# A layer of causal attention gated by an expert mixture: gating the last batch after the last head, weighing and gating on other engines, and adding the causal mask on VectorE

## The chip, the cores and the metric

The program runs on one core of one Trainium2 chip, in one launch. The metric is the device time of a launch in microseconds (us). The kernel before took 1059.01 us, the median of three runs (1058.56, 1059.01 and 1065.69). All times in the text are us unless marked ns.

A core has five engines with in-order streams that wait for each other only by semaphores: TensorE (PE; matmuls, results in PSUM), VectorE (DVE), ScalarE (ACT), GpSimd (POOL) and SyncE (SP, here a queue of DMAs). GpSimd can't reach PSUM.

## The reference, cut to what matters

```python
xn = layernorm(x)                              # x: 4 batches x 1024 tokens x 256
q  = (xn @ Wq + bq)  -> 8 heads of 128; k, v = xn @ Wkv + bkv    # one k, v for all heads
q, k += sinusoidal positions
scores = q k^T / sqrt(128); masked above the diagonal
s  = softmax(scores) v  -> 1024 x 1024, @ Wo   -> 1024 x 256 per batch
logits = xn @ router_w + router_b; the two largest of 8 experts are kept
f  = sum over the two kept experts of gate_e * (relu(xn @ w1[e] + b1[e]) @ w2[e] + b2[e])
out = x + s * silu(f)
```

## The kernel before, in words

**Two stages.** The first (to about 479 us) makes the layernorm, the routing and the eight experts; the experts' rows lie in device memory as `expert_outputs`. The second, `attention`, is the one that the change touches. It runs over 32 heads (4 batches x 8), n = 0 to 31. A token tile is 128 tokens; c = 0 to 31 are the tiles of all batches, c = 24 to 31 those of the last batch (`TILES` = 24).

**A head has five steps**, k = 5n + i. `GROUPS` says which query tiles u a step takes: (7), (6, 0), (5, 1), (4, 2), (3). Tile u needs (u + 1) x 128 columns of scores, so a head has eight blocks of 1024, 896 + 128, 768 + 256, 640 + 384 and 512 columns. The order of each engine's stream is written out by hand in loops over k:

- TensorE: `scores` (three matmul passes of f16 parts, and for the diagonal block a fourth matmul, L1346, that adds the mask: identity x `maskb`), then `values` of the head before, then in steps 0 and 2 a job (`project`, the q of head n + 2), and in step 4 `o_tile`, the output projection of tile n - 9. Heads 30 and 31 have no job.
- VectorE: `o_gated` (step 0, L1608), `job_positions` (L1551), `reciprocals` (L1571), `o_low` (steps 0 and 3, L1587), `maxima` (L1542), `job_low` (L1565), `low` of two steps back (L1581), and then `whole_f` (step 2, L1593) and `gated` (step 4, L1602).
- ScalarE: `job_high` (L1473), `high` of the step before (L1483), `expo` (L1453, with an accumulator read behind each block), `o_high` (steps 2 and 4, L1461), `weigh` (step 1, L1491) and `tanh` (step 3, L1509).
- GpSimd: `added` (step 1, L1664) and `fetch` (step 3, L1658), two indirect DMAs that gather the two expert rows of each token of a tile.
- SyncE: the transposing DMAs of the probabilities' two f16 parts, and loads and stores of x.

**Gating one tile** takes: `fetch` (two gathers), `weigh` (f = gate0 x row0), `whole_f` (f += gate1 x row1), `tanh` (of f / 2), `gated` (G = (tanh + 1) x f), `o_gated` (G x the tile's output projection) and `added` (+ x). `yg` has three buffers, `fb`, `thb` and `Gb` two. Before, the order `seq` takes the last batch's eight tiles first, one in each of heads 1 to 8 (they rest in `GD`), then tiles 0 to 23 in heads 9 to 31 and one behind the last head. The last batch's output projection is made after the last head in four PSUM banks (`rows_out`, L1399), multiplied by `GD` in `closing` (L1635), added to x and stored.

## Time and profile before

| | before |
|---|---|
| median of 3 runs | 1059.01 us |
| the profiled execution's own time | 1065.57 us |
| its span, first to last instruction | 1063.7 us |
| TensorE busy, share of the span | 992.4 us, 93% |
| VectorE busy | 859.3 us, 81% |
| ScalarE busy | 647.2 us, 61% |
| GpSimd busy | 339.2 us, 32% |
| mean granted TensorE clock | 0.996 |

The page's shares are means over the two stages, whose limits differ, so the stretches of the attention stage are read one by one. A "head" is counted below from the start of one reduction over 1024 columns (step 0) to the next. A row's duration of an instruction overlaps the next one's start by some 0.1 us on VectorE and ScalarE; where the text speaks of a step, it is the distance from start to start.

### The profile page before, as it was taken

How to read it: one execution, taken by the hardware profiler on the slowest of the kernel's cores; microseconds unless marked ns; L12 is line 12 of the kernel's file. 1: busy time of each engine (PE TensorE's matmuls, PEld its weight loads, DVE VectorE, ACT ScalarE, POOL GpSimd, SP SyncE). 2: the span in 40 equal slices, each digit the busy share in tenths (PEclk: the TensorE clock that was granted, in tenths of full speed). 3: DMA queues.
4: the chain of work that ended last, by engine and by line, in shares of the span. 5: the costliest groups of instructions: out<-in, count | busy, mean ns of one | idle time of the engine just before them, and what ended most of it. 6: DMA issues, size and time to landing. Idle time of an engine off the chain costs nothing.

```text
span 1063.7 us, 25358 instructions
## 1 busy us (share of the span) xinstructions
PE 992.4 (93%) x8590; PEld 774.2 (73%) x8590; DVE 859.3 (81%) x1529; ACT 647.2 (61%) x1370; POOL 339.2 (32%) x350
## 2 busy tenths in 40 slices
PE   0797999999999999999988989999999999999997
PEld 0565888888888888886655656777777777777776
DVE  6986578787676546559999999999999999999972
ACT  2743233333332333338888988888888888888860
POOL 3104899899997300002110101212121111212111
PEclk9999899999999999999999999999999999999999
DMA  8777687768775522218989999999999998999992
GB/s 277 228 287 154 164 204 191 203 179 198 175 174 160 155 46 67 62 45 187 178 158 188 159 159 170 190 185 187 173 185 180 188 179 174 168 161 164 180 176 91
DMA packets 428269, 179.46 MB, mean 169 GB/s; under 512 B 363850, under 2 KB 417940, under 8 KB 427380
## 3 DMA queue, kind: packets, MB, share of 16 engines
q1 hardware_dynamic: 364272, 131.39, 60.5%
q10 hardware_dynamic: 57396, 28.74, 11.4%
q0 software_dynamic: 6480, 17.70, 6.4%
q8 instruction: 77, 1.26, 0.5%
q14 instruction: 44, 0.36, 0.1%
HBM read 54.94 MB, written 34.87 MB: 84 GB/s over the span
## 4 chain that ended last, share of the span: by engine, by line
PE 36%; DVE 11%; ACT 4%; issue 3%; ACTq 0%; DVEq 0%
PE b_psS L1343 11%; PE b_psO L1371 11%; PE b_psJ L1388 5%; PE b_psJ L1302 5%; DVE b_ph L1581 4%; DVE b_nmax L1542 4%; PE b_psS L1399 2%; ACT b_pr L1453 2%; ACT b_ph L1483 1%; PE b_psO L1374 1%; DVE b_psJ L1551 1%; PE b_psS L1346 1%; DVE b_Q L1565 1%; DVE b_outs L1587 1%; ACT b_outs L1461 0%
## 5 line engine op out<-in xcount | busy, mean ns | idle before, releaser
L1005 PE MATMUL psU<-bxT,w_p 128*128 128x256 f16 (+1 forms) x1920 | 288.0, 262 | 10.7 <-DMA bxT<-expert_rows 4.9
L1096 ACT ACTIVATE h<-psU,bias 128x256 f32<-128x256 f32 (+1 forms) x320 | 123.9, 449 | 257.4 <-PE psU L1005 205.2
L1014 PE MATMUL psY<-w_p,hp 128*128 x1704 | 274.9, 274 | 0.1
L1343 PE MATMUL b_psS<-b_kp,b_Q 128*128 128x512 f16 (+3 forms) x1152 | 218.6, 326 | 12.3 <-ACT b_pr L1453 10.8
L1453 ACT ACTIVATE b_pr<-b_psS,b_nmax 128x1024 f32<-128x1024 f32 (+7 forms) x256 | 187.0, 735 | 43.9 <-DVE b_nmax L1542 42.9
L1005 PEld LDWEIGHTS psU<-bxT,w_p 128*128 x1920 | 187.3, 98 | 34.4 <-issue 15.5
L1371 PE MATMUL b_psO<-b_pT,b_vp 128*128 128x256 f16 x1536 | 202.9, 273 | 1.2 <-DVE b_Q L1565 0.9
L1581 DVE SCALAR_TENSOR_TENSOR b_ph<-b_pr,b_rrec,b_ph 128x1024 f16<-128x1024 f32 (+7 forms) x256 | 199.3, 810 | 0.0
L1483 ACT ACTIVATE b_ph<-b_pr,b_rrec 128x1024 f16<-128x1024 f32 (+7 forms) x256 | 187.0, 768 | 13.8 <-DVE b_rrec L1571 13.8
L1124 DVE CAST hp<-h 128x512 f16<-128x512 f32 (+1 forms) x160 | 92.3, 577 | 125.5 <-ACT h L1096 125.4
L1542 DVE TENSOR_REDUCE b_nmax<-b_psS 128x1 f32<-128x1024 f32 (+7 forms) x256 | 183.1, 746 | 5.1 <-PE b_psS L1346 2.6
L1014 PEld LDWEIGHTS psY<-w_p,hp 128*128 128x128 f16 x1704 | 166.7, 98 | 21.9 <-issue 1.0
L1343 PEld LDWEIGHTS b_psS<-b_kp,b_Q 128*128 128x128 f16 x1152 | 102.4, 98 | 90.8 <-ACT b_pr L1453 14.5
L1371 PEld LDWEIGHTS b_psO<-b_pT,b_vp 128*128 128x128 f16 x1536 | 140.7, 98 | 19.7 <-DVE b_Q L1565 1.1
L1658 POOL DMA_INDIRECT b_yg<-expert_outputs,pos x64 | 68.4, 1070 | 240.3 <-DMA expert_outputs<-y 118.2
L1664 POOL TENSOR_TENSOR b_x_row<-b_G,b_x_row 128x256 f32<-128x256 f32 x24 | 17.5, 730 | 351.2 <-DVE b_G L1608 343.4
L1126 DVE TENSOR_TENSOR hp<-h,hp 128x512 f16<-128x512 f32 (+1 forms) x160 | 125.1, 782 | 5.5
L191 POOL DMA_INDIRECT rowx<-xn_split,who x71 | 78.1, 1099 | 72.1 <-DVE who L864 46.3
L1388 PE MATMUL b_psJ<-b_wo,b_outs 128*128 128x256 f16 x576 | 66.8, 273 | 0.8 <-DVE b_Q L1565 0.8
L280 POOL TENSOR_TENSOR w_p<-wstage,w_p 128x512 f16<-128x512 f32 x48 | 65.8, 1371 | 4.1
L1374 PE MATMUL b_psO<-b_pT,b_vp 128*128 128x128 f16 x384 | 61.5, 219 | 0.0
L1388 PEld LDWEIGHTS b_psJ<-b_wo,b_outs 128*128 128x128 f16 x576 | 55.3, 98 | 7.3 <-DVE b_Q L1565 1.0
(191 smaller groups left out, 1041.1 us busy)
## 6 DMA issues: line engine op xcount, KB each, us to landing
wstage<-in_L_ffn_w SPq DMA_DIRECT2D x48, 256.0 KB, 3.3
expert_rows<-rowx SPq DMA_DIRECT2D x67, 128.0 KB
expert_outputs<-y ACTq DMA_DIRECT2D x31, 256.0 KB, 3.2
b_pT<-b_ph SPq DMA_TRANSPOSE x320, 3.4
a_x_all<-in_L_attn_x SPq DMA_DIRECT2D x8, 512.0 KB, 9.7
...
```

Of the source, the lines that this page charges most:

```text
L1005: mm = eng.matmul(psU[w % U][:, g % 2, 0:tiles * P].rearrange("p (t r) -> p t r", t=tiles), weight(n, a * W1 + c * H + g * P, P), bxT[n % ...
L1014: mm = eng.matmul(psY[n % 2][:, t, :], hp[n % 2][:, a, g, t * P:(t + 1) * P], weight(n, 2 * W1 + (2 * g + b) * D, D), start=(g == 0 and k ...
L1096: a = eng.activation(h32[w % 4][:, g, 0:rows], psU[w % U][:, g, 0:rows], ACT.Relu, bias=bias[:, ds(e * HT + 2 * q + g, 1)], scale=1.0 / WS)
L1124: eng.tensor_copy(hi, full).then_inc(hh_, 1)
L1126: eng.tensor_tensor(lo, full, hi, ALU.subtract).then_inc(hl_, 1)
L1343: mm = eng.matmul(dst, Q[n % 3][:, a, u * P:(u + 1) * P], kb[:, c, lo:lo + w], start=(kk == 0), stop=(kk == 2 and not last))
L1371: eng.matmul(both, vb[:, a, j, :], pT[:, at + j:at + j + hop + 1:hop, :], start=(c == 0 and j == 0 and a == 0), stop=False)
L1388: mm = eng.matmul(psJ[:, 0:D], outs[b % many][:, a, h, t * P:(t + 1) * P], wo_p[:, e, h, :], start=(h == 0 and kk == 0), stop=(h == HEADS ...
L1453: a = eng.activation(pr[k % 3][:, o:o + w], psS[BUF[i]][:, :, :].rearrange("p a n -> p (a n)")[:, o:o + w], ACT.Exp, bias=nmax[:, at:at + ...
L1483: a = eng.activation(ph[k % 4][:, o:o + w], pr[k % 3][:, o:o + w], ACT.Copy, scale=rrec[:, at:at + 1])
L1542: a = eng.tensor_reduce(nmax[:, at:at + 1], psS[BUF[i]][:, :, :].rearrange("p a n -> p (a n)")[:, o:o + w], AX.X, ALU.max, negate=True)
L1581: a = eng.scalar_tensor_tensor(ph[k % 4][:, first + o:first + o + w], pr[k % 3][:, o:o + w], rrec[:, at:at + 1], ph[k % 4][:, o:o + w], AL ...
```

## The change

- `seq` now takes tiles 0 to 23 first. Nothing is fetched, weighed or gated in heads 1 to 8. The eight tiles of the last batch (`ENDING`) are fetched, weighed and gated behind tile 23, after the last head: ScalarE weighs and takes the tanh, VectorE adds and gates.
- For tiles 0 to 23, in heads 9 to 31 and just behind, ScalarE weighs both rows (two instructions where one was), GpSimd makes the sum (`whole_f`), adds one to the tanh and multiplies (`gated`); VectorE does neither.
- In heads 10 to 30 (`BANDED`) TensorE leaves out the mask matmul. VectorE's reduction becomes `tensor_tensor_reduce`: it reads the scores from PSUM and `band` from SBUF, writes -(scores + band) back to PSUM and keeps the minimum. ScalarE's exponential takes the block with scale -1.

```diff
+LARGEST = 3.4028234e38
+BANDED = range(10, 31)
...
-    seq = list(range(TILES, NT)) + list(range(TILES))
+    LEAD = HEADS + 1
+    ENDING = [TILES + 2 * j + i for j in PAIRS for i in range(2)]
+    seq = list(range(TILES)) + ENDING
...
+        band = sb("band", [P, T], BF16)
...
-                        last = lo + w == w_all
+                        last = lo + w == w_all and n not in BANDED
...
-                                       bias=nmax[:, at:at + 1], accum_out=rsum[:, at:at + 1])
+                                       bias=nmax[:, at:at + 1], scale=-1.0 if k // 5 in BANDED else 1.0, accum_out=rsum[:, at:at + 1])
...
-                eng.activation(fb[s % 2][:, :], yg[s % 3][:, 0, :], ACT.Copy, scale=gate[:, 0, c:c + 1]).then_inc(u0_, 1)
+                eng.activation(fb[s % 2][:, :], yg[s % 3][:, 0, :], ACT.Copy, scale=gate[:, 0, c:c + 1])
+                eng.activation(yg[s % 3][:, 1, :], yg[s % 3][:, 1, :], ACT.Copy, scale=gate[:, 1, c:c + 1]).then_inc(u0_, 1)
...
-                if k < LAST and n:
+                if k < LAST and n >= LEAD:
                     if i == 1:
-                        weigh(seq[n - 1])
+                        weigh(n - LEAD)
                     if i == 3:
-                        tanh(seq[n - 1])
+                        tanh(n - LEAD)
             weigh(TILES - 1)
             tanh(TILES - 1)
             for half in range(2):
+                ending = ENDING[4 * half:4 * half + 4]
+                weigh(ending[0])
+                for x, c in enumerate(ending):
+                    if x < 3:
+                        weigh(ending[x + 1])
+                    tanh(c)
                 o_high(NH - 1, half)
...
-                    a = eng.tensor_reduce(nmax[:, at:at + 1], psS[BUF[i]][:, :, :].rearrange("p a n -> p (a n)")[:, o:o + w],
-                                          AX.X, ALU.max, negate=True)
+                    s = psS[BUF[i]][:, :, :].rearrange("p a n -> p (a n)")[:, o:o + w]
+                    if k // 5 in BANDED:
+                        a = eng.tensor_tensor_reduce(s, s, band[:, T - w:T], -1.0, LARGEST, ALU.add, ALU.min, nmax[:, at:at + 1])
+                    else:
+                        a = eng.tensor_reduce(nmax[:, at:at + 1], s, AX.X, ALU.max, negate=True)
...
-                eng.scalar_tensor_tensor(fb[s % 2][:, :], yg[s % 3][:, 1, :], gate[:, 1, c:c + 1], fb[s % 2][:, :],
-                                         ALU.mult, ALU.add).then_inc(f_, 1)
+                eng.tensor_tensor(fb[s % 2][:, :], yg[s % 3][:, 1, :], fb[s % 2][:, :], ALU.add).then_inc(f_, 1)
...
-                if k < LAST and n:
-                    if i == 2:
-                        whole_f(seq[n - 1])
-                    if i == 4:
-                        gated(seq[n - 1])
...
-            whole_f(TILES - 1)
-            gated(TILES - 1)
+            def ending(half):
+                tiles = ENDING[4 * half:4 * half + 4]
+                whole_f(tiles[0])
+                for x, c in enumerate(tiles):
+                    if x < 3:
+                        whole_f(tiles[x + 1])
+                    gated(c)
+
             o_gated(TILES - 1)
+            ending(0)
             o_low(NH - 1, 0)
+            ending(1)
             closing(0)
...
+            def whole_f(c):
+                s = turn_of[c]
+                eng.wait_ge(u0_, s + 1)
+                eng.tensor_tensor(fb[s % 2][:, :], yg[s % 3][:, 1, :], fb[s % 2][:, :], ALU.add).then_inc(f_, 1)
+
+            def gated(c):
+                s = turn_of[c]
+                eng.wait_ge(th_, s + 1)
+                eng.tensor_scalar(thb[s % 2][:, :], thb[s % 2][:, :], 1.0, 1.0, ALU.add, ALU.mult).then_inc(t1_, 1)
+                if c >= 2:
+                    eng.wait_ge(oa_, c - 1)
+                eng.wait_ge(t1_, s + 1)
+                eng.tensor_tensor(Gb[c % 2][:, :], thb[s % 2][:, :], fb[s % 2][:, :], ALU.mult).then_inc(G_, 1)
...
+                if k < LAST and n >= LEAD:
+                    if i == 2:
+                        whole_f(n - LEAD)
+                    if i == 4:
+                        gated(n - LEAD)
+                if i == 3 and LEAD <= n + 1 < NH:
+                    fetch(n + 1 - LEAD)
+            fetch(TILES - 1)
+            whole_f(TILES - 1)
+            gated(TILES - 1)
             added(TILES - 1)
+            for c in ENDING:
+                fetch(c)
```

Three places show how the streams differ. **VectorE, from the end of step 3 of a head to step 0 of the next** (`b_psJ,b_G` is `o_gated`, `b_th,b_f` is `gated`, `b_outs` is `o_low`), before:

```order
L1542 TENSOR_REDUCE b_nmax<-b_psS 128x1 [waits b_scores]
L1581 SCALAR_TENSOR_TENSOR b_ph_22758<-b_pr_22773,b_rrec,b_ph_22758 128x768 [waits b_turned_lo1,b_p_hi]
L1581 SCALAR_TENSOR_TENSOR b_ph_22758<-b_pr_22773,b_rrec,b_ph_22758 128x256
L1602 SCALAR_TENSOR_TENSOR b_G_22768<-b_th_22766,b_f_22764 128x256 [waits b_o_added,b_f_tanh]
L1608 SCALAR_TENSOR_TENSOR b_G_22768<-b_psJ,b_G_22768 128x256 [waits b_o_rows,b_f_gated]
L1571 RECIPROCAL b_rrec<-b_rsum 128x1 [waits b_exponentials]
L1587 SCALAR_TENSOR_TENSOR b_outs_22771<-b_psO,bias,b_outs_22771 128x512 [waits b_o_hi]
L1542 TENSOR_REDUCE b_nmax<-b_psS 128x1 [waits b_scores]
```

and after:

```order
L1557 ISA b_psS,b_nmax<-b_psS,b_band 128x512 [waits b_scores]
L1557 ISA b_nmax 128x1
L1597 SCALAR_TENSOR_TENSOR b_ph_22759<-b_pr_22775,b_rrec,b_ph_22759 128x768 [waits b_turned_lo2,b_p_hi]
L1597 SCALAR_TENSOR_TENSOR b_ph_22759<-b_pr_22775,b_rrec,b_ph_22759 128x256
L1623 SCALAR_TENSOR_TENSOR b_G_22769<-b_psJ,b_G_22769 128x256 [waits b_o_rows,b_f_gated]
L1587 RECIPROCAL b_rrec<-b_rsum 128x1 [waits b_exponentials]
L1603 SCALAR_TENSOR_TENSOR b_outs_22771<-b_psO,bias,b_outs_22771 128x512 [waits b_o_hi]
L1557 ISA b_psS,b_nmax<-b_psS,b_band 128x1024 [waits b_scores]
L1557 ISA b_nmax 128x1
```

The gate is gone from the stream, and each reduction is now two instructions, the second of which writes `b_nmax`. **ScalarE in step 1 of a head** (`b_pr` is the exponential, `b_f` the weighing, `b_ph` is `high`), before:

```order
L1453 ACTIVATE b_pr_22775,b_rsum<-b_psS,b_nmax 128x128
L1504 DMA b_kp_22754<-later_kv 128x2x256 [waits kv_stored2,kv_stored1,kv_stored0]
L1491 ACTIVATE b_f_22765<-b_yg_22762,gate 128x256 [waits b_f_gated,b_y_in1]
L1483 ACTIVATE b_ph_22758<-b_pr_22775,b_rrec 128x896 [waits b_turned_hi1,b_reciprocals]
L1483 ACTIVATE b_ph_22758<-b_pr_22775,b_rrec 128x128
```

and after:

```order
L1459 ACTIVATE b_pr_22773,b_rsum<-b_psS,b_nmax 128x128
L1503 DMA b_xTb_other<-xn_turned 128x512
L1497 ACTIVATE b_f_22764<-b_yg_22762,gate 128x256 [waits b_f_gated,b_y_in1]
L1498 ACTIVATE b_yg_22762<-b_yg_22762,gate 128x256
L1489 ACTIVATE b_ph_22757<-b_pr_22773,b_rrec 128x896 [waits b_turned_hi0,b_reciprocals]
L1489 ACTIVATE b_ph_22757<-b_pr_22773,b_rrec 128x128
```

A second weighing stands between the exponential and `high`. **GpSimd at the end of the program**, after (before, nothing stood between the last two `b_x_row` and `b_x_last`):

```order
L1698 TENSOR_TENSOR b_x_row_22751<-b_G_22769,b_x_row_22751 128x256 [waits b_x_in2,b_o_gated]
L1678 DMA b_yg_22761<-expert_outputs,pos 128x256 [waits b_f_whole]
L1678 DMA b_yg_22761<-expert_outputs,pos 128x256
L1678 DMA b_yg_22762<-expert_outputs,pos 128x256 [waits b_f_whole]
L1678 DMA b_yg_22762<-expert_outputs,pos 128x256
L1678 DMA b_yg_22763<-expert_outputs,pos 128x256 [waits b_f_whole]
L1678 DMA b_yg_22763<-expert_outputs,pos 128x256
```

Sixteen gathers, two a tile, stand behind the last `added`.

## Rows read from the trace of the kernel before

**Rows 1.** Stretches of the attention stage: length, each engine's busy time, clock, DMA.

```profile
513.15:632.98 119.83, 107.23 (x823) 72.05 (x821) 113.60 (x204) 102.53 (x210) 11.37 (x12) 1.00 0.94 168
632.98:684.62 51.64, 48.84 (x392) 34.88 (x390) 49.77 (x91) 44.21 (x90) 6.45 (x7) 1.00 0.97 175
684.62:998.12 313.50, 313.50 (x2521) 226.93 (x2520) 300.37 (x541) 267.62 (x541) 53.79 (x55) 1.00 0.97 177
998.12:1013.98 15.86, 15.86 (x136) 12.02 (x135) 14.35 (x27) 13.48 (x29) 2.95 (x4) 1.00 1.04 190
```

**Rows 2.** Timeline of VectorE in one early head: start, length, instruction, idle before.

```profile
564.50 1.22 DVE L1542 TENSOR_REDUCE b_nmax<-b_psS 128x1 f32<-128x1024 f32 x1
...
566.95 0.69 DVE L1551 SCALAR_TENSOR_TENSOR b_psJ<-b_psJ,pe_sb 128x512 f32<-128x512 f32 x1
...
574.31 0.75 DVE L1587 SCALAR_TENSOR_TENSOR b_outs<-b_psO,bias,b_outs 128x512 f16<-128x512 f32 x1
...
578.15 0.15 DVE L1571 RECIPROCAL b_rrec<-b_rsum 128x2 f32<-128x2 f32 x1
...
580.95 0.75 DVE L1587 SCALAR_TENSOR_TENSOR b_outs<-b_psO,bias,b_outs 128x512 f16<-128x512 f32 x1 [0.33 <-ACT b_outs L1461]
```

**Rows 3.** Timeline of ScalarE in the same head.

```profile
567.68 0.69 ACT L1473 ACTIVATE b_Q<-b_psJ,bias 128x512 f16<-128x512 f32 x1 [0.72 <-DVE b_psJ L1551]
...
570.63 0.51 ACT L1491 ACTIVATE b_f<-b_yg,gate 128x256 f32<-128x256 f32 x1
571.03 1.33 ACT L1483 ACTIVATE b_ph<-b_pr,b_rrec 128x896 f16<-128x896 f32 x2
...
573.58 0.70 ACT L1461 ACTIVATE b_outs<-b_psO,bias 128x512 f16<-128x512 f32 x1
...
578.34 1.33 ACT L1483 ACTIVATE b_ph<-b_pr,b_rrec 128x640 f16<-128x640 f32 x2 [0.30 <-DVE b_rrec L1571]
...
580.25 0.67 ACT L1461 ACTIVATE b_outs<-b_psO,bias 128x512 f16<-128x512 f32 x1
```

**Rows 4.** Timeline of VectorE in a head of the long middle stretch.

```profile
822.85 0.42 DVE L1608 SCALAR_TENSOR_TENSOR b_G<-b_psJ,b_G 128x256 f32<-128x256 f32 x1
```

**Rows 5.** Groups by form in one middle head: busy us, mean ns.

```profile
L1453 ACT ACTIVATION_READ_ACCUMULATOR b_pr<-b_psS,b_nmax 128x1 f32 x8 | 1.6, 196 | 0.0
...
L1551 DVE SCALAR_TENSOR_TENSOR b_psJ<-b_psJ,pe_sb 128x512 f32<-128x512 f32 x2 | 1.4, 691 | 0.0
...
L1542 DVE TENSOR_REDUCE b_nmax<-b_psS 128x1 f32<-128x512 f32 x1 | 0.7, 671 | 0.0
...
L1571 DVE RECIPROCAL b_rrec<-b_rsum 128x1 f32<-128x1 f32 x2 | 0.3, 153 | 0.0
```

**Rows 6.** VectorE groups at 180 to 340 us, then at 410 to 478 us.

```profile
L1126 DVE TENSOR_TENSOR hp<-h,hp 128x512 f16<-128x512 f32 x60 | 57.8, 963 | 2.1
...
L1126 DVE TENSOR_TENSOR hp<-h,hp 128x512 f16<-128x512 f32 x16 | 11.1, 692 | 0.6
```

**Rows 7.** Timeline of GpSimd: first and last of six gathers, and the last `added`.

```profile
479.30 0.94 POOL L1658 DMA_INDIRECT b_yg<-expert_outputs,pos  x1 [118.22 <-DMA expert_outputs<-y]
...
485.56 0.95 POOL L1658 DMA_INDIRECT b_yg<-expert_outputs,pos  x1 [0.30 <-issue]
...
1037.79 0.72 POOL L1664 TENSOR_TENSOR b_x_row<-b_G,b_x_row 128x256 f32<-128x256 f32 x1 [7.78 <-DMA b_x_row<-in_L_attn_x]
```

**Rows 8.** The instructions of line L1658, the gathers.

```profile
DMA to landing us min/median/max: 2.9/3.9/6.0
```

**Rows 9.** The chain of waits at the end: start, length, engine and line.

```profile
1041.97 5.89 PE b_psS L1399 x54
```

**Rows 10.** Timeline of VectorE at the end.

```profile
1056.10 1.35 DVE L1635 SCALAR_TENSOR_TENSOR b_G_last<-b_psS,b_G_last 128x512 f32<-128x512 f32 x2 [3.77 <-PE b_psS L1399]
1057.55 1.13 DVE L1649 TENSOR_TENSOR b_x_last<-b_G_last,b_x_last 128x512 f32<-128x512 f32 x1
```

**Rows 11.** A stretch behind an idle TensorE, columns as in Rows 1.

```profile
106.00:108.00 2.00, 0.53 (x3) 0.44 (x4) 1.93 (x5) 0.24 (x1) 0.00 (x0) 0.50 1.28 141
```

More of the change, by code:

```diff
@@ L1277, in attention @@
         kl_, vl_ = sem("k_in"), sem("v_in")
+        bd_ = sem("band_laid")
         yl = [sem(f"y_in{i}") for i in range(3)]
@@ L1280, in attention @@
         xo = [sem(f"x_out{i}") for i in range(3)]
-        u0_, f_, th_, G_, ot_, oa_, xf_, fo_, fl_, wol = map(sem, (
-            "f_first", "f_whole", "f_tanh", "f_gated", "o_gated", "o_added", "x_last_in", "last_out", "last_pair_out", "wo_in"))
+        u0_, f_, th_, t1_, G_, ot_, oa_, xf_, fo_, fl_, wol = map(sem, (
+            "f_weighed", "f_whole", "f_tanh", "f_tanh_one", "f_gated", "o_gated", "o_added", "x_last_in", "last_out", "last_pair_out", "wo_in"))
         block = ctx.enter_context(nc.Block())
@@ L1619, in _ @@
                     o_low((k - 1) // 5 - 1, (k - 1) % 5 // 4)
+                if k == 5 * BANDED[0]:
+                    eng.wait_ge(bd_, 2)
                 if k < LAST:
@@ L1664, in added @@
                 eng.tensor_tensor(xr[c % 3][:, :], Gb[c % 2][:, :], xr[c % 3][:, :], ALU.add).then_inc(oa_, 1)
+            eng.memset(band[:, 0:T - P], 0.0).then_inc(bd_, 1)
+            eng.tensor_copy(band[:, T - P:T], maskb[:, :]).then_inc(bd_, 1)
             for i, o in enumerate(v["y_o"]):
@@ L1671, in _ @@
                     added(n - HEADS - 2)
-                if i == 3 and n < NH:
-                    fetch(seq[n])
+                if k < LAST and n >= LEAD:
[8 more added lines that the diff above has]
+            gated(TILES - 1)
             added(TILES - 1)
+            for c in ENDING:
+                fetch(c)
             eng.wait_ge(xf_, 16)
```

## The prediction, made before the changed kernel was run

> **What bounds the kernel now.** The page's shares mix two stages, so the first view is the table of stretches [rows 1]. It splits the attention stage by the start of each head. Heads 2 to 8 take 119.83 / 7 = 17.12 us each; heads 9 to 11 take 51.64 us together; the 18 heads 12 to 29 take 313.50 / 18 = 17.42 each; head 30 takes 15.86. In the third row TensorE is busy all 313.50 us, so those heads run at TensorE's pace. In the first row it is busy 107.23 of 119.83, and VectorE 113.60: neither is full, and a head still takes 17.12. Something else sets the pace there, and it must be found, since it is the floor that a lighter TensorE would fall to.
>
> The timelines of one such head show it [rows 2, 3]. I follow the head backwards through instructions that started as soon as their releaser was done, and write the steps from start to start. VectorE: reduction 564.50 to position sum 566.95, 2.45. ScalarE idles 0.72 for that sum and starts at 567.68, 0.73. ScalarE then runs without a gap: 2.95 to the weighing at 570.63, **0.40 for the weighing**, 2.55 to the o half at 573.58. VectorE takes over at 574.31, 0.73, and runs without a gap through the reductions of step 3 to the reciprocals at 578.15, 3.84. ScalarE had idled 0.30 for these and starts at 578.34, 0.19; 1.91 to its o half at 580.25; VectorE had idled 0.33 for it and starts at 580.95, 0.70; 0.67 to the next head's reduction. The sum is 2.45 + 0.73 + 2.95 + 0.40 + 2.55 + 0.73 + 3.84 + 0.19 + 1.91 + 0.70 + 0.67 = 17.12, exactly the head. So a loop that changes four times between VectorE and ScalarE sets these heads, although each has idle time elsewhere. In the middle heads this loop is still there, 0.30 under TensorE's 17.42.
>
> **The change, term by term.** The sum is made against the profiled execution, 1065.57 us (span 1063.7); the median of the runs is 6.6 below it, and I carry the difference over to the median.
>
> *Mask matmuls.* Eight a head leave TensorE. 54 matmuls of 256 columns take 5.89 us at the end [rows 9], 0.109 each, so one of 128 columns takes 0.0545 and eight 0.44. TensorE's need falls from 17.42 to 16.98. That is below the loop's 17.12, so at most 0.30 of it counts even if the loop stays as it is.
>
> *The second weighing.* It stands right behind the first, in ScalarE's gapless part of the loop [rows 3]: plus 0.40 a head.
>
> *The masked reduction.* The trace has none, so I bound it. Its main part has the operands of the position sum (PSUM in and out, one SBUF input): 691 ns at 512 columns against 671 for the reduction, plus 0.02 [rows 5]. The order shows a second instruction that writes one column. VectorE's own smallest is the reciprocal, 153 ns long, of which some 0.07 are not overlapped by what follows; ScalarE's accumulator read is 196 long. I take 0.02 + 0.07 = 0.09 for each, since the reciprocal is the nearest row on the same engine; the ends are 0 (all hidden) and 0.22 (an unoverlapped 196 plus 0.02). Three of a head's eight lie on the loop (step 0's one, step 3's two): plus 0.27 a head, 0 to 0.66.
>
> *What VectorE loses.* The sum of step 2 lies where VectorE was ahead of ScalarE: it is off the loop and worth nothing. The gate lies between the reciprocals of step 3 and the o half, beside ScalarE's part of 2.80 (578.15 to 580.95), which stays. VectorE's own way there, with the o product of 0.42 [rows 4], was about 0.05 longer than this with the gate; without the gate it is about 2.5. Worth nothing again. GpSimd's three new operations are hidden: it was busy 3 us of a middle head [rows 1], and its gate is due only at the o product.
>
> So the loop becomes 17.12 + 0.40 + 0.27 = 17.79. Heads 12 to 29: 18 x (17.79 - 17.42) = **plus 6.7**. Heads 9 to 11: head 9 has only the second weighing, 17.52, and 17.52 + 2 x 17.79 = 53.1 against 51.64: **plus 1.5**. Head 30 has no jobs and another loop, with six of the reductions but without the gate: 0.40 + 6 x 0.09 - 0.45, **plus 0.5**. In heads 1 to 8 ScalarE loses its weighing, but then waits for the reciprocals as it does elsewhere, 0.30 [rows 3]: 8 x 0.1, **minus 0.8**. Heads together: plus 7.9; with the ends of the reduction, plus 2.5 to 16.
>
> *The end.* Before, the last `added` started at 1037.79, released by a load of x that stays where it is [rows 7]. Now 16 gathers follow it, from 1038.6. Six in a row started 6.26 apart from first to last, 1.25 each [rows 7], so the last starts at 1038.6 + 15 x 1.25 = 1057.4 and lands 3.9 later [rows 8], at 1061.3. Three buffers don't slow this much: a tile's round is about 7.8 against 3 x 2.5. Then, for that last tile: two weighings 0.9, sum, tanh and gate 0.4 to 0.5 each with their hand-overs, in all 2.3: 1063.6. Behind it in VectorE's stream stand two closings (1.3) [rows 10] and the o half (0.75), 1065.7, for which TensorE waits with 12 matmuls (1.3, and 0.2 to drain), 1067.2; one more closing, 1067.9, and the final add. That add started at 1057.55 before [rows 10]: **plus 10.3**. The first four tiles also hold up the first o half, and TensorE stands idle from about 1046.5 (42 matmuls behind 1041.97 [rows 9]) to 1054.6 (eighth gather at 1047.4, 3.9, 2.3, and 1.0 for ScalarE's half); its remaining 9 us end near 1063.6, just under cover of the gating. At 106 us, behind such a gap, the granted clock is 0.50, the lower level of 1.2 GHz [rows 11]; 4 us of that work at that level would end 2 later, which the cover holds. With landings of 2.9 to 6.0 and the clock, the end costs 8 to 14.
>
> Sum: 7.9 + 10.3 = 18.2. Profiled execution 1083.8, median 1059.0 + 18.2 = **1077 us**.
>
> **A port that VectorE and GpSimd share.** VectorE's subtraction L1126, with two inputs in SBUF, has a mean of 963 ns while GpSimd computes and 692 while it doesn't [rows 6]. The new GpSimd operations can meet VectorE's `low`, which has two such inputs. I take nothing for it in the sum, because they fall beside step 2's and step 4's instructions, off the loop, with about 0.3 of slack; the rival below prices more. The Trainium skill, SBUF — State Buffer, section "SBUF: two separate sides", calls the port pair an exclusive lock in which the loser waits for the whole instruction; the stretching above agrees, and by that rule each of the three could hold `low` for up to its own 0.7.
>
> **Rivals.**
> 1. *The masked reduction is dear.* At 0.22 each the heads cost 16, the end 10.3: 1085. If it ran at half rate, the 2048 columns on the loop would add over 2 us a head and give 1120; the position sum, with the same operands, runs at full rate. Chances 0.11 and 0.04.
> 2. *GpSimd holds VectorE.* Step 4's two operations start when the tanh ends, as `low` runs. If one slips between its two blocks, `low` waits some 0.73, VectorE's branch there is 3.2 against 2.8, and a head costs 0.4 more: 20 heads, 8 more, 1085. It decides from 0.3 of stall on. 0.10.
> 3. *Not slower.* The loop isn't what holds the early heads, but VectorE's load of 16.2. Then the second weighing is hidden, heads 12 to 29 fall to TensorE's 16.98 (minus 7.9), the early heads gain up to 8 x 0.75 = 6, and with the end's 10.3 the time is 1055; with the end at 8, 1053. The place is ScalarE's stretch from 567.68 to 573.58; it decides if an idle gap of 0.4 opens there. Against it: the sum of 17.12 and TensorE's idle time in those heads. 0.10.
>
> The forecast has 0.65. A measurement of this kernel can't tell less than about 1% (10.6 us) from no change. Faster by over 1% would need rival 3 and an end at half price: 0.03. Within 1%: the rest of rival 3 and the lowest corner of both bounds, 0.09. Slower: 0.88. The range goes from the low ends of the heads and the end, 2.5 + 8, rounded down for the runs' own spread, 1068, to rivals 1 and 2 with the 6.6 by which runs differ, 1092.
>
> **What would show it.** Heads 12 to 29 at 17.7 to 17.9 each, with TensorE no longer full; the early heads at 17.0 to 17.1; ScalarE gapless from step 0's job to its o half, with two weighings of 0.4 in it; VectorE's second instruction near 0.07 from start to start; sixteen gathers 1.25 apart behind the last `added`; TensorE idle some 8 us near the end. Wrong would be heads at 17.0 (rival 3), a masked reduction over 0.2 longer than the old one (rival 1), or `low` stretched in step 4 (rival 2).

## The result, and the profile after

The changed kernel takes 1081.64 us, the median of four runs (1077.3 to 1082.48). The kernel before took 1061.05 in four runs beside them (1058.56 to 1065.69). The ratio is 1.0147, with an interval from 1.0104 to 1.0191: slower by 1.5%. The profiled execution took 1081.56 (span 1079.7), 16.0 more than that of before. The median stands 4.6 above the forecast of 1077 and inside the range. By the ratio's interval the change costs 11 to 20 us, and the 16.0 of the two profiled executions lie in the middle of it; the two medians of four runs each are 20.6 apart, just above its upper end.

The two profiled executions, cut at the same places (us, from the starts of the reductions over 1024 columns):

| piece | before | after | difference | predicted |
|---|---|---|---|---|
| start to head 1 | 494.43 | 494.12 | -0.3 | 0 |
| head 1 | 18.72 | 18.32 | -0.40 | -0.1 |
| heads 2 to 8, each | 17.12 | 17.07 | -0.37 for seven | -0.7 for seven |
| heads 9 to 11 | 51.64 | 52.74 | +1.10 | +1.5 |
| heads 12 to 29, each | 17.417 | 17.617 | +3.60 for 18 | +6.7 for 18 |
| head 30 | 15.86 | 16.57 | +0.71 | +0.5 |
| head 31 to the final add | 43.57 | 55.31 | +11.74 | +10.3 |
| behind it | 6.12 | 6.12 | 0.0 | 0 |
| span | 1063.7 | 1079.7 | +16.0 | +18.2 |

So the end is most of it, and a little larger than predicted, and the heads are a little over half of what was predicted. The same four stretches as in [rows 1], after the change, and one stretch near the end:

```profile
512.44:631.90 119.46, 107.22 (x825) 72.31 (x824) 109.69 (x190) 97.60 (x196) 0.00 (x0) 1.00 0.90 155
631.90:684.64 52.74, 48.89 (x377) 33.91 (x376) 49.66 (x102) 44.94 (x93) 15.90 (x18) 1.00 0.94 174
684.64:1001.74 317.10, 311.52 (x2379) 216.99 (x2377) 299.01 (x650) 270.71 (x559) 96.77 (x109) 1.00 0.97 175
1001.74:1018.31 16.57, 15.98 (x137) 12.13 (x135) 14.30 (x33) 13.92 (x30) 5.99 (x7) 1.00 1.01 169
1054.00:1058.00 4.00, 0.00 (x0) 0.00 (x0) 1.17 (x4) 2.42 (x6) 3.08 (x4) 0.53 0.32 98
```

In the third row TensorE, full before, now has 5.6 us without work: it no longer sets the pace. VectorE has 1.4 less work than before in these heads and ScalarE 3.1 more, and neither is near 317. In the first row the early heads lost 3.9 us of VectorE's work and 4.9 of ScalarE's and became 0.4 shorter in all.

The loop of [rows 2, 3] in one middle head after the change, first VectorE (start, length, instruction, idle before):

```profile
825.57 1.22 DVE L1557 CUSTOM_DVE_ANT_0 b_psS<-b_psS,b_band 128x1024 f32<-128x1024 f32 x1
826.71 0.13 DVE L1557 DVE_READ_ACCUMULATOR2_ANT b_nmax<- 128x1 f32 x1
826.71 1.40 DVE L1597 SCALAR_TENSOR_TENSOR b_ph<-b_pr,b_rrec,b_ph 128x640 f16<-128x640 f32 x2
828.04 0.69 DVE L1567 SCALAR_TENSOR_TENSOR b_psJ<-b_psJ,pe_sb 128x512 f32<-128x512 f32 x1
...
835.78 0.75 DVE L1603 SCALAR_TENSOR_TENSOR b_outs<-b_psO,bias,b_outs 128x512 f16<-128x512 f32 x1 [0.41 <-ACT b_outs L1467]
...
839.69 0.16 DVE L1587 RECIPROCAL b_rrec<-b_rsum 128x2 f32<-128x2 f32 x1
839.76 0.68 DVE L1557 CUSTOM_DVE_ANT_0 b_psS<-b_psS,b_band 128x512 f32<-128x512 f32 x1
840.36 0.14 DVE L1557 DVE_READ_ACCUMULATOR2_ANT b_nmax<- 128x1 f32 x1
840.36 1.85 DVE L1597 SCALAR_TENSOR_TENSOR b_ph<-b_pr,b_rrec,b_ph 128x768 f16<-128x768 f32 x2
842.13 0.41 DVE L1623 SCALAR_TENSOR_TENSOR b_G<-b_psJ,b_G 128x256 f32<-128x256 f32 x1
842.47 0.15 DVE L1587 RECIPROCAL b_rrec<-b_rsum 128x1 f32<-128x1 f32 x1
842.54 0.73 DVE L1603 SCALAR_TENSOR_TENSOR b_outs<-b_psO,bias,b_outs 128x512 f16<-128x512 f32 x1
843.19 1.22 DVE L1557 CUSTOM_DVE_ANT_0 b_psS<-b_psS,b_band 128x1024 f32<-128x1024 f32 x1
```

then ScalarE's part of it:

```profile
828.76 0.69 ACT L1479 ACTIVATE b_Q<-b_psJ,bias 128x512 f16<-128x512 f32 x1 [0.67 <-DVE b_psJ L1567]
...
831.71 0.51 ACT L1497 ACTIVATE b_f<-b_yg,gate 128x256 f32<-128x256 f32 x1
832.11 0.50 ACT L1498 ACTIVATE b_yg<-b_yg,gate 128x256 f32<-128x256 f32 x1
832.51 1.33 ACT L1489 ACTIVATE b_ph<-b_pr,b_rrec 128x896 f16<-128x896 f32 x2
...
835.06 0.69 ACT L1467 ACTIVATE b_outs<-b_psO,bias 128x512 f16<-128x512 f32 x1
```

and GpSimd in step 4:

```profile
839.72 0.41 POOL L1689 TENSOR_SCALAR b_th<-b_th 128x256 f32<-128x256 f32 x1 [3.07 <-ACT b_th L1516]
840.27 0.73 POOL L1693 TENSOR_TENSOR b_G<-b_th,b_f 128x256 f32<-128x256 f32 x1
```

The loop is the predicted one, but for step 4, where the way now goes through VectorE's own 2.85 and the prediction had ScalarE's 2.80 beside it. Start to start: 2.47 + 0.72 + 2.95 + 0.80 for two weighings (831.71 to 832.51) + 2.55 + 0.72 + 3.91 (835.78 to 839.69) + 2.85 (839.69 to 842.54) + 0.65 = 17.62, the head. The 0.40 of the second weighing is there in full. VectorE's two stretches with reductions on the loop grew by 0.02 (2.47 for 2.45) and 0.07 (3.91 for 3.84): 0.09 for three masked reductions, 0.03 each, where 0.09 each was predicted. (In the mean of heads 12 to 29 the two stretches are 2.467 and 3.908, and 2.454 and 3.843 in `mask_back`, below, whose reductions are the plain ones: 0.08.) The accumulator read is 0.13 long, but the next instruction starts at the very time at which it starts (826.71, 837.19 in the same way, 840.36), so its place in the stream costs nothing that can be seen.

The end, on GpSimd:

```profile
1036.62 0.96 POOL L1678 DMA_INDIRECT b_yg<-expert_outputs,pos  x1 [0.30 <-issue]
...
1042.76 0.73 POOL L1693 TENSOR_TENSOR b_G<-b_th,b_f 128x256 f32<-128x256 f32 x1
1044.02 0.72 POOL L1698 TENSOR_TENSOR b_x_row<-b_G,b_x_row 128x256 f32<-128x256 f32 x1 [0.54 <-DVE b_G L1623]
1044.90 1.01 POOL L1678 DMA_INDIRECT b_yg<-expert_outputs,pos  x1 [0.15 <-issue]
...
1064.35 0.95 POOL L1678 DMA_INDIRECT b_yg<-expert_outputs,pos  x1 [0.30 <-issue]
```

on ScalarE, when the last tile's rows have landed, and TensorE before its last work:

```profile
1067.12 0.51 ACT L1497 ACTIVATE b_f<-b_yg,gate 128x256 f32<-128x256 f32 x1 [1.32 <-DMA b_yg<-expert_outputs,pos]
```

```profile
1059.88 2.74 PE L1405 MATMUL b_psS<-b_wo,b_outs 128*128 128x256 f16 x12 [9.01 <-DVE b_outs L1603]
```

and on VectorE, to the final add:

```profile
1068.40 0.99 DVE L1617 SCALAR_TENSOR_TENSOR b_G_last<-b_th,b_f 128x256 f32<-128x256 f32 x2
1069.31 1.28 DVE L1647 SCALAR_TENSOR_TENSOR b_G_last<-b_psS,b_G_last 128x512 f32<-128x512 f32 x2
1070.50 0.74 DVE L1603 SCALAR_TENSOR_TENSOR b_outs<-b_psO,bias,b_outs 128x512 f16<-128x512 f32 x1
1072.17 1.35 DVE L1647 SCALAR_TENSOR_TENSOR b_G_last<-b_psS,b_G_last 128x512 f32<-128x512 f32 x2 [0.92 <-PE b_psS L1405]
1073.62 1.13 DVE L1669 TENSOR_TENSOR b_x_last<-b_G_last,b_x_last 128x512 f32<-128x512 f32 x1
```

Sixteen gathers behind the last `added`, the last 19.45 after the first (1.30 each), and behind its landing the predicted chain of gate, closings, o half, matmuls, closing and final add. TensorE stands idle for 9.01 us (some 8 were predicted). The granted clock of 1054 to 1058 is 0.53, near the lower level of 1.2 GHz; it reads 0.50 from 1056 to 1064, and TensorE starts again at 1059.88, so its next 4 us run at that level, as foretold.

### The profile page after: what moved, and what is told of

Its sections match the earlier page's. It is cut to its first block, busy times and chain, and to the rows that moved or that the text cites. A ratio compares the mean times of both kernels' runs of the same rounds, so it can differ in the third digit from the quotient of the medians.

```text
span 1079.7 us, 25249 instructions
## 1 busy us (share of the span) xinstructions
PE 990.7 (92%) x8422; PEld 762.6 (71%) x8422; DVE 862.8 (80%) x1649; ACT 656.2 (61%) x1402; POOL 399.3 (37%) x424
## 4 chain that ended last, share of the span: by engine, by line
DVE 27%; ACT 17%; issue 8%; POOL 2%; PE 1%; DMA 1%; ACTq 0%; DVEq 0%; POOLq 0%
DVE b_ph L1597 10%; ACT b_pr L1459 7%; DVE b_psS L1557 6%; ACT b_ph L1489 6%; DVE b_nmax L1559 3%; ACT b_outs L1467 2%; DVE b_outs L1603 2%; DVE b_Q L1581 2%; DVE b_psJ L1567 2%; POOL b_yg L1678 2%; ACT b_yg L1498 1%; DVE b_G L1623 1%; ACT b_f L1497 1%; DMA b_yg<-expert_outputs,pos 1%; DVE b_rrec L1587 1%
## 5 line engine op out<-in xcount | busy, mean ns | idle before, releaser
L1349 PE MATMUL b_psS<-b_kp,b_Q 128*128 128x512 f16 (+3 forms) x1152 | 215.0, 326 | 13.1 <-ACT b_pr L1459 11.7
L1597 DVE SCALAR_TENSOR_TENSOR b_ph<-b_pr,b_rrec,b_ph 128x1024 f16<-128x1024 f32 (+7 forms) x256 | 210.6, 853 | 0.0
L1126 DVE CAST hp<-h 128x512 f16<-128x512 f32 (+1 forms) x160 | 94.7, 592 | 121.1 <-ACT h L1098 120.8
L1377 PEld LDWEIGHTS b_psO<-b_pT,b_vp 128*128 128x128 f16 x1536 | 144.0, 98 | 24.0 <-DVE b_Q L1581 1.1
L1128 DVE TENSOR_TENSOR hp<-h,hp 128x512 f16<-128x512 f32 (+1 forms) x160 | 129.8, 811 | 5.5
L1684 POOL TENSOR_TENSOR b_f<-b_yg,b_f 128x256 f32<-128x256 f32 x24 | 17.5, 730 | 312.5 <-ACT b_yg L1498 312.5
L1557 DVE CUSTOM_DVE_ANT_0 b_psS<-b_psS,b_band 128x1024 f32<-128x1024 f32 (+7 forms) x168 | 123.6, 766 | 0.0
L1678 POOL DMA_INDIRECT b_yg<-expert_outputs,pos x64 | 81.3, 1270 | 15.9 <-issue 12.2
L1559 DVE TENSOR_REDUCE b_nmax<-b_psS 128x1 f32<-128x1024 f32 (+3 forms) x88 | 62.8, 745 | 2.6 <-PE b_psS L1352 2.6
```

Source lines behind the costliest of these rows:

```text
L1128: eng.tensor_tensor(lo, full, hi, ALU.subtract).then_inc(hl_, 1)
L1349: mm = eng.matmul(dst, Q[n % 3][:, a, u * P:(u + 1) * P], kb[:, c, lo:lo + w], start=(kk == 0), stop=(kk == 2 and not last))
L1377: eng.matmul(both, vb[:, a, j, :], pT[:, at + j:at + j + hop + 1:hop, :], start=(c == 0 and j == 0 and a == 0), stop=False)
L1557: a = eng.tensor_tensor_reduce(s, s, band[:, T - w:T], -1.0, LARGEST, ALU.add, ALU.min, nmax[:, at:at + 1])
L1597: a = eng.scalar_tensor_tensor(ph[k % 4][:, first + o:first + o + w], pr[k % 3][:, o:o + w], rrec[:, at:at + 1], ph[k % 4][:, o:o + w], AL ...
L1678: eng.indirect_dma_start(yg[s % 3][:, i, :], None, y_d, bass.IndirectOffsetOnAxis(ap=pos[:, i, c:c + 1], axis=0)).then_inc(yl[s % 3], 16)
```

## The experiments

Each is read by the same cuts. "Each" is a head of 12 to 29; "the end" is head 31's start to the final add.

| kernel | heads 2 to 8, each | heads 9 to 11 | each | head 30 | the end | span |
|---|---|---|---|---|---|---|
| before | 17.12 | 51.64 | 17.417 | 15.86 | 43.57 | 1063.7 |
| after | 17.07 | 52.74 | 17.617 | 16.57 | 55.31 | 1079.7 |
| mask_only | 17.12 | 51.71 | 17.278 | 16.20 | 43.56 | 1064.1 |
| order_only | 17.06 | 51.64 | 17.417 | 15.85 | 55.30 | 1077.0 |
| one_weighing | 17.06 | 51.58 | 17.247 | 16.20 | 54.32 | 1066.5 |
| mask_back | 17.07 | 52.55 | 17.525 | 16.25 | 56.64 | 1077.8 |
| end_earlier | 17.06 | 52.73 | 17.616 | 16.57 | 50.40 | 1074.6 |
| gpsimd_more | 17.05 | 53.98 | 18.031 | 17.18 | 57.23 | 1090.7 |
| early_only | 16.75 | 51.27 | 17.417 | 15.84 | 43.56 | 1055.3 |
| mask_early | 16.74 | 50.90 | 17.112 | 16.18 | 44.42 | 1054.7 |

Between executions the stretch up to head 1, which no experiment changes, differs by up to 8 us (489.05 to 496.88), while the heads of unchanged parts agree within 0.01. So the lengths of heads are the finer measure, and spans differ by that first stretch too. The end is a coarser one: in `after`, `order_only`, `one_weighing`, `mask_back` and `gpsimd_more`, which all fetch the last batch behind the last `added`, it lies between 54.3 and 57.2.

### mask_only: the mask on VectorE alone

```diff
 # before, with these alone
+BANDED = range(10, 31)
-                        last = lo + w == w_all
+                        last = lo + w == w_all and n not in BANDED
+                    if k // 5 in BANDED:
+                        a = eng.tensor_tensor_reduce(s, s, band[:, T - w:T], -1.0, LARGEST, ALU.add, ALU.min, nmax[:, at:at + 1])
```

> The kernel before with one part of the change: VectorE adds the mask in heads 10 to 30, TensorE leaves it out; weighing, gating and order as before. Loop theory (the VectorE-ScalarE loop of 17.12 us sets a head once TensorE falls to 16.98): heads 12 to 29 take 17.12 plus 0.05 for VectorE's branch with gate and o product plus 3 or 4 times 0.03 for the masked reductions, 17.25 to 17.3 each, against 17.42; the whole 2 to 3 us faster than before. Rival, the masked reduction is what made the heads of the changed kernel longer: heads at 17.5 or more and the whole slower than before. Rival, TensorE sets the pace: heads at 16.98 and the whole 8 us faster.

Measured: heads 12 to 29 take 17.278 each. The median is 1058.95 beside 1064.71 of the kernel before, ratio 0.9957 [0.9923, 0.9991].

```profile
687.16:998.17 311.01, 309.81 (x2379) 217.18 (x2377) 301.39 (x685) 266.15 (x541) 53.01 (x55) 1.00 0.98 179
```

TensorE was relieved of 142 matmuls (2521 in the third row of [rows 1], 2379 here), priced at 0.44 a head, and the head became 0.14 shorter. The loop theory had this: the loop of VectorE and ScalarE stands at 17.28 and takes the rest. TensorE's records leave only 1.20 of the stretch without work, so this run alone doesn't exclude that TensorE still sets the pace; `mask_early`, below, does, with the same matmuls in heads of 17.112. Head 30 became 0.34 longer.

### order_only: the last batch behind the last head, all engines as before

```diff
 # before, with these alone
-    seq = list(range(TILES, NT)) + list(range(TILES))
+    LEAD = HEADS + 1
+    ENDING = [TILES + 2 * j + i for j in PAIRS for i in range(2)]
+    seq = list(range(TILES)) + ENDING
```

(and the loops behind the last head; one row is weighed by ScalarE, VectorE makes the sum and the gate as before.)

> The kernel before with another part of the change alone: the last batch's tiles are fetched, weighed and gated behind the last head, by the engines of before (one weighing on ScalarE, sum and gate on VectorE); mask on TensorE. Theory (the end is set by the sixteen gathers, 1.25 us apart): heads 12 to 29 stay at 17.42, heads 1 to 8 gain 0.8 us in all, and from the start of head 31 to the final add it takes 11 to 12 us more than before; the whole 10 to 11 us slower than before. Rival (the end was long because of the doubled weighing and GpSimd's gate): the end costs 6 us or less.

Measured: the end takes 55.30, for 43.57 before and 55.31 after; heads 12 to 29 stay at 17.417; head 1 loses 0.40 and each of the other early heads 0.06. 1075.09 beside 1064.71, ratio 1.0105 [1.0072, 1.0139]. So most of the end's cost belongs to the order, and the rival (6 us or less) is out. That the two ends are equal to 0.01 is luck, as their parts show:

| | head 31's start to the last `added` | to the last gather's start | until ScalarE has its rows | to the final add |
|---|---|---|---|---|
| order_only | 24.4 | 20.4 | 4.4 | 6.2 |
| after | 25.7 | 20.3 | 2.8 | 6.5 |

```profile
1039.95 0.72 POOL L1682 TENSOR_TENSOR b_x_row<-b_G,b_x_row 128x256 f32<-128x256 f32 x1 [5.58 <-DVE b_G L1616]
```

Here the last `added` starts 2.47 behind the weighing of its rows (1037.48), in the changed kernel 4.06 behind it (1039.96 to 1044.02), since two weighings and three GpSimd operations stand between: 1.6 of the end belong to the engines. The longer landing of the last gather, 4.4 for 2.8, made up for it in this execution.

### one_weighing: the change without the second weighing

```diff
 # after, without
-                eng.activation(yg[s % 3][:, 1, :], yg[s % 3][:, 1, :], ACT.Copy, scale=gate[:, 1, c:c + 1]).then_inc(u0_, 1)
```

The second expert's row goes into the sum unweighed here.

> The changed kernel without the second weighing on ScalarE (the second expert's row goes into the sum unweighed; all else is computed). Loop theory: heads 12 to 29 fall by the 0.40 us of that instruction, from 17.62 to 17.2 or 17.25, the whole 7 to 8 us faster than the changed kernel. Rival (the reductions, or the port that GpSimd and VectorE share, make the heads 17.62): heads stay within 0.1 us of 17.62.

Measured: 17.247 each, 0.37 less than after, and 1069.0 beside 1064.71, ratio 1.0049 [1.0013, 1.0084].

```profile
679.38:989.82 310.44, 309.30 (x2379) 217.16 (x2377) 296.44 (x649) 264.03 (x541) 81.99 (x109) 1.00 0.98 179
```

ScalarE's work fell from 270.71 to 264.03 over 18 heads, 0.37 a head, and the head became as much shorter. This is the test of the loop: in the changed kernel ScalarE has 2.6 us without work in each head, and 0.4 of work still costs 0.4, since it stands where ScalarE is the one that is waited for.

### mask_back: the change with the mask on TensorE again

```diff
 # after, with
-BANDED = range(10, 31)
+BANDED = range(0)
```

> The changed kernel with the mask back on TensorE in all heads and the plain reduction on VectorE; two weighings, GpSimd's gate and the late batch stay. Loop theory: the loop loses 0.03 to 0.1 us for the three reductions on it and stands at 17.5 to 17.6, just over TensorE's 17.42, so the whole is 0 to 2 us faster than the changed kernel. Rival (the masked reduction costs 0.09 us each, as predicted): heads at 17.42 or below 17.45, the whole 4 us faster.

Measured: 17.525 each, 0.09 less than after; 1079.94 beside 1064.71, ratio 1.0148 [1.0078, 1.0219], where that of after is 1.0147: the whole can't tell the two apart, and the heads can. With the mask on TensorE the loop is 17.12 + 0.40 = 17.52 and TensorE's 17.42 no longer matters, and the three reductions on the loop are worth 0.08 to 0.09 together (the stretches above; VectorE's way in step 4 gives another 0.05 and the step to the next reduction takes 0.03 back).

### end_earlier: the last batch's first gathers moved ahead

```diff
 # after, GpSimd's stream, with
+                if i == 3 and LEAD <= n + 1 <= NH:
+                    fetch(n + 1 - LEAD)
...
+            for c in ENDING[:2]:
+                fetch(c)
             whole_f(TILES - 1)
             gated(TILES - 1)
             added(TILES - 1)
-            for c in ENDING:
+            for c in ENDING[2:]:
                 fetch(c)
```

> The changed kernel with tile 23's gathers back in head 31 and the first two of the last batch's tiles fetched before tile 23 is summed, so that 12 gathers instead of 16 stand behind the last added row and tile 23's own two no longer stand in the end. Theory (the gathers' pace of 1.25 to 1.3 us and their late start set the end): last gather some 7 us earlier, from the start of head 31 to the final add 48 to 49 us instead of 55.3; heads unchanged. Rival (TensorE at the lower clock and its rows behind the gating set the end): 53 us or more.

Measured: the end takes 50.40, 4.9 less; 7 were expected, and the rival's 53 or more is out. 1078.33 beside 1065.06, ratio 1.0119 [1.0059, 1.0179].

```profile
1039.86 0.74 POOL L1684 TENSOR_TENSOR b_f<-b_yg,b_f 128x256 f32<-128x256 f32 x1
...
1044.09 0.73 POOL L1698 TENSOR_TENSOR b_x_row<-b_G,b_x_row 128x256 f32<-128x256 f32 x1 [1.67 <-DMA b_x_row<-in_L_attn_x]
...
1059.05 0.95 POOL L1678 DMA_INDIRECT b_yg<-expert_outputs,pos  x1 [0.31 <-issue]
```

Counted from head 31's start, the last gather starts 5.1 earlier and the end is 4.9 shorter, so the gathers and what they queue behind set the end. The 2 us that were missing lie before the last `added`, behind which twelve gathers queue: it started no earlier than in the change (1044.02). Two things held it. Tile 23's sum stands behind the four gathers in GpSimd's stream and starts at 1039.86, though its rows were weighed at 1034.42, so VectorE's product for it comes at 1042.45, only 1.07 earlier than in the change (1043.52). Then `added`, which starts 0.50 behind that product in the change, waited here until 1044.09 for the load of x. The expectation had taken both to be out of the way.

### gpsimd_more: one more GpSimd operation in step 4

```diff
 # after, in GpSimd's gated, ahead of the tensor_scalar
+                eng.tensor_tensor(spare[:, :], thb[s % 2][:, :], fb[s % 2][:, :], ALU.mult).then_inc(sp_, 1)
+                eng.wait_ge(sp_, s + 1)
```

> The changed kernel with one more GpSimd product per tile in heads (same size as its gate, written to a spare tile, right before the tanh plus one). Port theory: GpSimd's operations in step 4 hold VectorE's subtraction there; with 0.73 us more of them the subtraction stretches by a further 0.3 to 0.7 us, VectorE's branch is the one that is waited for, and heads 12 to 29 go from 17.62 to 17.9 to 18.3. Rival (GpSimd is hidden): heads stay at 17.62, since its own stream has 10 us of idle time a head.

Measured: 18.031 each, 0.41 more than after; 1096.62 beside 1065.06, ratio 1.0304 [1.024, 1.0368]. The size is the expected one, the way only partly. Step 4 of a middle head, VectorE and GpSimd in order of time:

```profile
844.60 1.55 DVE L1599 SCALAR_TENSOR_TENSOR b_ph<-b_pr,b_rrec,b_ph 128x768 f16<-128x768 f32 x2
844.76 1.11 POOL L1693 TENSOR_SCALAR b_th<-b_th 128x256 f32<-128x256 f32 x1
846.02 0.72 POOL L1697 TENSOR_TENSOR b_G<-b_th,b_f 128x256 f32<-128x256 f32 x1
846.78 0.42 DVE L1625 SCALAR_TENSOR_TENSOR b_G<-b_psJ,b_G 128x256 f32<-128x256 f32 x1 [0.64 <-POOL b_G L1697]
```

Here the hold went mostly the other way: `low` (two instructions) is 1.55 long, where it is 1.41 with nothing beside it, and GpSimd's addition to the tanh is 1.11 instead of 0.41, so that the gate comes late and VectorE's o product idles 0.64 for it. In the changed kernel GpSimd's product starts just before `low` (840.27 and 840.36) and `low` is the longer one; here `low` starts first (844.60 and 844.76) and GpSimd's is. The added product (0.73) decided which of the two came first.

### early_only: the position sum taken off the loop

The loop of [rows 2] passes from the reduction over 1024 columns through `low` to the position sum that ScalarE's step 2 of the loop waits for. Moved ahead of `low`, the sum is made 1.3 sooner, until another way to ScalarE's step is the longer one.

```diff
 # before, VectorE's stream, with
+            def early(k):
+                return k >= 10 and k % 5 == 0 and k in jobs.at
-                if k - 1 in jobs.at:
+                if k - 1 in jobs.at and not early(k - 1):
                     job_positions(jobs.at[k - 1])
...
+                if early(k):
+                    job_positions(jobs.at[k])
                 low(k - 2)
```

> The kernel before with one step moved on VectorE: from head 2 on, the position sum of step 0's job stands before that step's subtraction instead of behind it, 1.3 us earlier, so ScalarE can take it in its idle time. Loop theory: it leaves the loop, and heads 2 to 8 fall from 17.12 to 16.7 to 16.8; heads 12 to 29 stay at TensorE's 17.42; in all 2 to 3 us faster than before. Rival (the early heads are set by VectorE's load of 16.2 plus waits of its own, and no loop): they stay at 17.1.

Measured: heads 2 to 8 take 16.746 each, for 17.119; heads 12 to 29 stay at 17.417. 1063.12 beside 1065.06, ratio 0.9975 [0.9937, 1.0013]: the gain is too small for a run's time, and plain in the heads.

```profile
507.75:624.97 117.22, 106.97 (x819) 71.71 (x817) 113.57 (x205) 103.24 (x210) 11.33 (x12) 1.00 0.95 171
```

Every engine has the work that it had in the first row of [rows 1] within 1%, and the stretch is 2.6 shorter. Only the order of two VectorE instructions differs: the loop set the early heads, and TensorE sets the middle ones.

### mask_early: both, as a version to keep

`mask_only` with the edit of `early_only`.

> The same move together with the mask on VectorE in heads 10 to 30, the rest as before. Loop theory: the floor under TensorE is now below 16.98, so heads 12 to 29 fall from 17.42 to 17.0 to 17.05, heads 2 to 8 to 16.75, head 31 and the end stay: 10 to 11 us faster than before, ratio 0.990. Rival (another wait takes the place of the one removed): heads 12 to 29 at 17.2 or more, the whole less than 6 us faster.

Measured: 1056.66, the median of eleven runs, beside 1065.06, ratio 0.9901 [0.9864, 0.9938]. It is faster than both kernels. The heads 12 to 29 take 17.112 each, above the 17.0 to 17.05 expected, and the end 44.42, 0.9 more than before, which the expectation didn't have. The trace shows where it lies: TensorE's last idle time is for a transposing DMA of the probabilities:

```profile
1010.17 0.27 PE L1375 MATMUL b_psO<-b_pT,b_vp 128*128 128x256 f16 x1 [0.69 <-DMA b_pT<-b_ph]
```

The scores behind it start at 1010.34, 6.2 behind head 31's start, where before they start 5.4 behind it (1019.36), at the end of TensorE's last idle time; from there TensorE works without a gap in both. Why the transposed part came late was not tried. The heads, and one of them on VectorE:

```profile
679.94:987.95 308.01, 307.02 (x2378) 217.78 (x2376) 302.26 (x686) 268.07 (x541) 47.43 (x55) 1.00 1.01 180
```

```profile
834.42 1.22 DVE L1548 CUSTOM_DVE_ANT_0 b_psS<-b_psS,b_band 128x1024 f32<-128x1024 f32 x1
...
835.56 0.73 DVE L1558 SCALAR_TENSOR_TENSOR b_psJ<-b_psJ,pe_sb 128x512 f32<-128x512 f32 x1
836.20 1.40 DVE L1591 SCALAR_TENSOR_TENSOR b_ph<-b_pr,b_rrec,b_ph 128x640 f16<-128x640 f32 x2
```

The sum now stands right behind the reduction, at 835.56. TensorE's records read 307.02 of 308.01, or 17.06 a head, where the prediction's own need of it was 16.98. These records hold waits too: the same matmuls (2378 or 2379 of them) read 311.52 in the changed kernel, 309.81 in `mask_only`, 309.30 in `one_weighing` and 307.02 here. So TensorE's need is at most 17.06 a head, VectorE has 302.26 of work in the 308.01, and what sets the 17.11 stays open.

## Why the prediction came out as it did

**The loop was right.** That its steps add up to the head proves nothing by itself: distances from start to start add up along any chain that ends where it began. What makes it a loop is that each step starts without idle time or when the step before it releases it, and what tests it are changes on it and beside it. It was read from [rows 2, 3] before the change and predicted that 0.40 of ScalarE's work would cost 0.40 a head although ScalarE was idle for a seventh of it. Head 9, which has the second weighing alone, was predicted at 17.52 and took 17.52 (631.90 to 649.42). `one_weighing` takes 0.37 of it away again, `mask_back` shows 17.525, and `early_only` shortens the early heads by 0.37 without removing any work. Rival 3, in which VectorE's load sets the early heads, falls with this: with the gating gone from them VectorE had 3.9 us less work over seven heads, and they gave 0.37 in all.

**The masked reduction was mis-sized.** The term was 0.09 for each of three on the loop. It measured 0.03: 0.02 and 0.07 more in the two stretches that hold one and two of them, and 0.09 a head between `mask_back` and after, 0.08 of it in these stretches. The main part was right, 679 ns at 512 columns for 671 [rows 5]; what failed was the step that gave the accumulator read the reciprocal's unoverlapped 0.07:

```profile
L1557 DVE DVE_READ_ACCUMULATOR2_ANT b_nmax<- 128x1 f32 x8 | 1.1, 139 | 0.0
...
L1557 DVE CUSTOM_DVE_ANT_0 b_psS<-b_psS,b_band 128x512 f32<-128x512 f32 x1 | 0.7, 679 | 0.0
```

It is 139 ns long and wholly under the next instruction. The stated lower end, "0 (all hidden)", was the case for it, and rival 1, a dear reduction, is out. The 0.03 is what these two cuts show; `mask_only` in head 30, at 0.34 for six, would allow 0.06. In the sum, 18 x 0.18 = 3.2 of the heads' 7.9 go with this and 0.4 more in heads 10 and 11; head 30 took 0.2 back, which leaves the heads' miss of 3.3. (By the prediction's own terms the low end of the heads is 1.9 and not 2.5: 1.8 + 0.9 - 0.05 - 0.8. Nothing else hangs on it.)

**The port holds VectorE, and the slack takes it.** The pair of `low` in step 4 is 1.85 long where it was 1.40 to 1.41, while GpSimd's product (840.27 to 841.00) runs beside it; its addition to the tanh (839.72 to 840.13) is over when `low` starts at 840.36. The prediction counted on about 0.3 of slack from the gate that VectorE no longer does, and the trace bears it out: VectorE's way from the reciprocals to the o half is 2.85 after (839.69 to 842.54) and was 2.85 before (the reciprocals at 820.41, the o half at 823.26 of the head of [rows 4]), since the hold of 0.44 took the place of the gate of 0.45. So rival 2's mechanism is there, at no more than some 0.05 a head (2.85 against ScalarE's 2.80). It decides only when GpSimd's part grows: `gpsimd_more` adds 0.41. The Trainium skill, SBUF — State Buffer, section "SBUF: two separate sides", has the loser of the port pair fully blocked until the winner's instruction is over. The two kernels agree that either engine can be the loser, the one that starts second (`low` by 0.44 in one, the tensor_scalar by 0.70 in the other). Whether it is blocked fully they don't show: `low` started 0.64 before the end of GpSimd's product and grew by 0.44. The profile shows it as a longer instruction and not as a wait.

**The end was right within 1.4.** Against the prediction's steps:

| step | predicted | measured |
|---|---|---|
| head 31's start to the last `added` | 23.8, as before (1013.98 to 1037.79) | 25.7 (1018.31 to 1044.02) |
| from there to the last gather's start | 19.6 | 20.3 |
| its landing | 3.9 | 2.8 (to 1067.12) |
| landing to the final add | 6.6 | 6.5 |

What failed is the first step, "released by a load of x that stays where it is": the load no longer releases it. The prediction had the last `added` wait for x alone, as before, where tile 23 had been fetched at 1014.30, 0.3 behind head 31's start, and was ready long before. The change moves tile 23's two gathers too, behind the `added` of head 31 (1034.01); the second starts at 1036.62, its rows are weighed from 1039.96, and gate (1042.76) and product (1043.52) follow. The last `added` is released by that product, as the row of 1044.02 above says. The load of x went out at 1039.98, 21.7 behind head 31's start, instead of 1035.24, 21.3 behind it. Its landing isn't in the changed kernel's trace; in `order_only` it is 2.4 behind the issue, and at that pace the load is no longer what the `added` waits for. On SyncE's queue, after and then before:

```profile
1039.98 0.58 SPq L1756 DMA_DIRECT2D b_x_row<-in_L_attn_x  x1
```

```profile
1035.24 0.58 SPq L1710 DMA_DIRECT2D b_x_row<-in_L_attn_x  x1
```

and in `end_earlier`:

```profile
1040.35 0.58 SPq L1757 DMA_DIRECT2D b_x_row<-in_L_attn_x  x1
```

In `end_earlier` the load is the releaser again: with tile 23's product 1.07 sooner its `added` still starts only at 1044.09, 3.7 behind the load's issue, where before it was 2.6 (1037.79). Why the load takes longer there was not tried; two gathers were issued just before it (1037.65 and 1038.90), and none before the change. The gathers' pace of 1.30 for 1.25 added 0.7 and the shorter landing took 1.1 back. TensorE's 9.01 us of idle time and the lower clock behind it were covered by the gating, as said, but only just: its work before the last 12 matmuls ends at 1071.12, and those wait, 0.19, for the o half that ends at 1071.24.

**The early heads and head 30.** Removing ScalarE's weighing from heads 1 to 8 gave 0.77 for 0.8 predicted, though unevenly: 0.40 in head 1 and 0.05 in each other. That 0.40 of work off the loop gives 0.05 there isn't against the loop, since ScalarE then waits for the reciprocals, as predicted. `order_only` gives the same (18.32 and 17.06), so it belongs to the order alone. Head 30 cost 0.71 for 0.5: the masked reductions 0.34 (`mask_only`, 16.20) where 0.54 was predicted, the second weighing 0.37. The absent gate, taken for -0.45, is worth nothing: `one_weighing` has no gate on VectorE there, `mask_only` has it, and both take 16.20. This step of the prediction failed twice over. A hold of 0.47 takes the place of the gate's 0.45; `low` in step 4 of head 30, in `mask_only` and in `one_weighing`:

```profile
1011.53 1.41 DVE L1588 SCALAR_TENSOR_TENSOR b_ph<-b_pr,b_rrec,b_ph 128x768 f16<-128x768 f32 x2
```

```profile
1003.16 1.88 DVE L1596 SCALAR_TENSOR_TENSOR b_ph<-b_pr,b_rrec,b_ph 128x768 f16<-128x768 f32 x2
```

And without the hold, ScalarE's way beside it, which the prediction counted in the middle heads and not here, leaves at most some 0.1 to gain, by an estimate from its 2.80 in those heads: VectorE's way here takes 2.88 (1002.49 to 1005.37).

**Two misses offset.** Heads 3.3 too high and the end 1.4 too low leave the sum 1.9 above, and the first stretch's 0.3 makes it 2.2 (18.2 for 16.0). The median of 1081.64 is above the forecast all the same: the forecast carried the profiled execution's distance to the median over, 6.6 us, and the changed kernel's profiled execution stood at its median. That distance is no property of the kernel, as the first stretch's 8 us from run to run show.

**Could the change gain?** Each part has its price now. The mask alone is worth 0.14 a head of the 0.44 taken to leave TensorE, since the loop stands right under it; the second weighing takes 0.34 back; the end costs 11.7, 1.6 of it by the engines and the rest by the order. What gains is shortening the loop first and then relieving TensorE, as `mask_early` does.
